# Expert numbers loaded two a slot behind up and down products, and matrix copies held until the up product of slot 10, in a two-stage mixture-of-experts kernel

## The reference

```python
def bitlinear(x, w):
    wq = w + jax.lax.stop_gradient(_weight_quant(w) - w)
    xq = x + jax.lax.stop_gradient(_act_quant(x) - x)
    return xq @ wq.T
...
idx = jnp.argmax(logits, axis=-1).reshape(-1)
for e in range(E):
    g = bitlinear(xf, wg[e])
    u = bitlinear(xf, wu[e])
    y = bitlinear(jnp.square(jax.nn.relu(g)) * u, wd[e])
    out = out + jnp.where((idx == e)[:, None], y, 0.0)
```

## Time and profile before

| | |
|---|---|
| median of three runs | 247.35 us (246.73 to 247.69) |
| the profiled execution | 247.17 us, of which the span of the profile is 245.3 us |
| busy in the span | TensorE 218.7 us (89%), VectorE 209.0 (85%), ScalarE 197.7 (81%), POOL 160.4 (65%) |
| first stage, up to the last product of block 18 | until about 169 us |
| loop over slots, gate 3 to gate 19 | about 182.6 to 232 us |
| last output write issued | 240.5 us |

### The profile page before, as it was taken

The page is one execution under the profiler, slowest core; times in us unless marked ns, Lnnn a source line. Parts: engine busy times, 40 slices in busy tenths (PEclk is TensorE's granted clock), DMA queues, the critical chain, the costliest instruction groups (busy, mean ns, idle before and its releaser), DMA issues.

```text
span 245.3 us, 6263 instructions
## 1 busy us (share of the span) xinstructions
PE 218.7 (89%) x1622; PEld 170.4 (69%) x1629; DVE 209.0 (85%) x696; ACT 197.7 (81%) x297; POOL 160.4 (65%) x324
## 2 busy tenths in 40 slices
PE   2398999999999999999999999987789999899970
PEld 2245688889899999999999998976334544343430
DVE  5969999977969899899988999979799998888771
ACT  2757799877768889998999979896678998788860
POOL 5262667756637598888987887553734878557762
PEclk9999999999999999999999999999979999999998
DMA  5999999996985266679565786335328899994120
GB/s 199 426 319 383 413 421 385 402 378 187 392 302 174 81 263 218 254 261 339 166 245 212 251 252 220 95 122 178 97 50 241 289 293 366 379 387 190 65 108 13
DMA packets 14273, 61.44 MB, mean 250 GB/s; under 512 B 2654, under 2 KB 2654, under 8 KB 9632
## 3 DMA queue, kind: packets, MB, share of 16 engines
q1 hardware_dynamic: 9600, 47.60, 53.6%
q0 software_dynamic: 4640, 13.44, 15.6%
HBM read 43.88 MB, written 12.70 MB: 231 GB/s over the span
## 4 chain that ended last, share of the span: by engine, by line
PE 68%; DVE 14%; DMA 7%; issue 6%; ACT 3%; POOL 1%; DVEq 0%; ACTq 0%; POOLq 0%
PE banks L1834 35%; PE banks L2014 15%; PE banks L1817 7%; DMA ternary<-weight_chunks 4%; PE banks L2016 4%; DMA x<-x_rows,gather 2%; PE banks L2003 2%; PE banks L1979 2%; PE banks L1859 2%; POOL out_rows L778 1%; DVE stats L1249 1%; DVE row L1305 1%; PE banks L1887 1%; DVE ternary L1108 1%; DVE p L1285 1%
## 5 line engine op out<-in xcount | busy, mean ns | idle before, releaser
L833 ACT ACTIVATE ternary<-staged 128x2048 bf16<-128x2048 f32 x20 | 38.1, 1906 | 1.8 <-DMA staged<-weight_chunks 1.8
L2014 PE MATMUL banks<-ternary,qT 128*128 x126 | 34.6, 394 | 3.3 <-ACT qT L922 1.6
L839 ACT ACTIVATE ternary<-staged,w_scale 128x1536 int16<-128x1536 f32 (+1 forms) x20 | 34.4, 1724 | 2.9 <-DVE w_scale L1202 2.9
L692 POOL DMA_INDIRECT x_rows<-row,store_at x19 | 22.3, 1172 | 9.3 <-POOL store_at L684 6.9
L1834 PE MATMUL banks<-ctx_hi,pT_hi 128*128 x132 | 23.0, 313 | 1.7 <-DVE row L1305 1.1
L594 POOL DMA_INDIRECT x<-x_rows,gather x16 | 18.3, 1145 | 9.2 <-DVE gather L1120 6.3
L647 POOL TENSOR_TENSOR row<-ln,half_powers 128x2 f32<-128x2 f32 x19 | 14.1, 744 | 14.9 <-DVE squares L1320 14.9
L2014 PEld LDWEIGHTS banks<-ternary,qT 128*128 128x128 bf16 x128 | 12.4, 101 | 16.4 <-issue 8.5
L1834 PE MATMUL banks<-ctx_hi,hT_hi 128*128 x132 | 22.8, 312 | 0.0
L1834 PE MATMUL banks<-ctx_lo,hT_hi 128*128 x132 | 21.2, 300 | 0.2 <-DVE ctx_lo L1149 0.2
L1834 PE MATMUL banks<-ctx_hi,pT_lo 128*128 x132 | 21.3, 301 | 0.0
(11 more groups left out here) (284 smaller groups left out, 641.0 us busy)
## 6 DMA issues: line engine op xcount, KB each, us to landing
staged<-weight_chunks SPq DMA_DIRECT2D x20, 1024.0 KB
twin<-ternary SPq DMA_DIRECT2D x4, 1536.0 KB
ternary<-ctx_chunks SPq DMA_DIRECT2D x4, 1024.0 KB, 7.9
ternary<-weight_chunks SPq DMA_DIRECT2D x4, 1024.0 KB, 12.3
ternary<-ctx_rows SPq DMA_DIRECT2D x4, 1024.0 KB, 11.0
late_rows<-x_rows SPq DMA_DIRECT2D x11, 260.0 KB, 3.0
x_rows<-filler SPq DMA_DIRECT2D x1, 2080.0 KB
staged<-x_rows SPq DMA_DIRECT2D x5, 260.0 KB, 3.5
```

The source lines that it names most:

```text
L692: pool.indirect_dma_start(x1_rows, bass.IndirectOffsetOnAxis(ap=store_at[b % ROWS][:, :], axis=0), row[b % ROWS][:, :], None, bounds_check ...
L833: nc.scalar.activation(ternary[:, m * K * D:(m + 1) * K * D], staged_of(i), ACT.Abs, accum_out=abs_sum[:, 2 * i:2 * i + 1]).then_inc(abs_r ...
L839: nc.scalar.activation(ternary[:, m * K * D + first:(m + 1) * K * D].bitcast(I16), staged_of(i)[:, first:], ACT.Copy, scale=w_scale[:, m:m ...
L2014: last = pe.matmul(ps[:, :], rows, ternary[:, columns], start=(k == 0), stop=(k == K - 1))
```

## The change

Three things are moved, none is added to the work.

1. `load_ffn_expert` leaves the gate products. In the loop over `u`, behind `up_product(u)` the number of slot u+1 is loaded for u < 5, and of slot 2u-3 from u = 5 on; behind `down_product(u-3)` that of slot 2u-2 is loaded from u = 4 on, and both only while there is such a slot. So slot 4 loads numbers 5 and 6, slots 5 to 10 load 7 to 18, two each, and slot 11 loads 19.
2. SP issues all eight half loads of slots 16 to 19 in a row, then loads the four numbers of the copies.
3. It then waits until `u_ready` is 11 (`NUMBERS`), which is when the up product of slot 10 is done, and issues the four copies one behind the other.

```diff
+NUMBERS = (B2 + EARLY) // 2 - 1
...
-            def copy_matrices(s):
+            def second_expert(s):
                 place = s - EARLY + SECOND
-                e = sp.value_load(expert2[1][place:place + 1, 0:1], min_val=0, max_val=E2 - 1)
+                return sp.value_load(expert2[1][place:place + 1, 0:1], min_val=0, max_val=E2 - 1)
+
+            def copy_matrices(s, e):
                 sp.dma_start(twin[s - SPLIT][:, :], ternary[:, bass.ds(e * (3 * K * D), 3 * K * D)])\
                     .then_inc(twin_in[s - SPLIT], 16)
...
             for s in range(SPLIT, B2):
                 for half in range(2):
                     load_half(s, half)
-                copy_matrices(s)
+            seconds = [second_expert(s) for s in range(SPLIT, B2)]
+            sp.wait_ge(u_ready, NUMBERS)
+            for s in range(SPLIT, B2):
+                copy_matrices(s, seconds[s - SPLIT])
...
             def gate_product(b):
...
-                ahead = None
-                if b >= EARLY:
-                    def ahead():
-                        load_ffn_expert(b + 1)
...
-                product2(g_ps[b % 2], qT[b % 2], b, 0, ahead=ahead).then_inc(g_ready, 1)
+                product2(g_ps[b % 2], qT[b % 2], b, 0).then_inc(g_ready, 1)
...
                 up_product(u)
-                if u < EARLY:
-                    load_ffn_expert(u + 1)
+
+                load_ffn_expert(u + 1 if u < EARLY else 2 * u - EARLY + 2)
                 if u == EARLY - 1:
                     spread_means(1)
                     transpose_q(u + 1)
                 transpose_r(u - 2)
                 down_product(u - 3)
+                if u >= EARLY - 1:
+                    load_ffn_expert(2 * u - EARLY + 3)
```

## The result

The changed kernel takes 249.75 us (median of 12 runs, 248.31 to 252.25); the kernel before, on the same chip, 247.07 (12 runs, 246.24 to 247.69). The ratio is 1.0113, 95% interval 1.0087 to 1.0138. 244.5 was forecast, so the time lies 3.5 us above the end of the range.

The account below looks back on a forecast made before the run. TensorE, 68% of the chain of waits, bounds the kernel, with stalls at number loads. 247.17 - 2.9 (stalls gone) + 0.1 (loads 18 and 19) = 244.4, 244.5 on the median's footing; range 243.9 to 246.2.

Parts of the forecast that it names:

- The excess at number loads: Gates 5 to 18: number loads, stretched by copies, leave 3.02 us of excess; moving them wins 2.9 us.
- They come back two a slot ... I take nothing: Behind up and down, slots 4 to 11: 14 loads of about 0.65 us hide under waits, cost nothing.
- My bounds, nothing and 0.20 a load: Moved number loads: nothing each by gates 6 to 8, 0.20 each by gate 5, 2.8 us in all.
- two loads a slot eat the lead: Rival, TensorE's instructions fall behind the array: 0.1 a load gives 245.9 us, 0.20 gives 247.3; chance 0.13.
- SP's row loads come together: SP: eight half loads at about 0.84 us end at 201.3, four numbers by 203.1 to 204.1.
- The copies must be there in time: SP's queue: 6.29 MB at 262 to 325 GB/s end between 223.7 and 228.3, all hidden, 0.3 to 5 us spare.
- the last copy is late: Rival: the fourth copy ends at 230.3, gate 19 waits 1.7 us, time 246.2; chance 0.07.
- In order: SP's queue: the four copies land one after another, each a quarter of the span after the one before.
- sharing of the queue: Rival: four copies share SP's queue, the first lands with the last, gate 16 stands 5 to 9 us, 250 to 253; chance 0.03.
- The wait for slot 10: SP reaches its wait just as up product 10 ends; nothing but the copies stands behind it.
- the cases for "faster": Below 246.1 us: all hidden (0.73), two thirds of the first rival, half of the second; given as 0.84.

Follow-up runs that it names:

- e9: Changed kernel without the four copies and TensorE's wait for them, second halves reading fixed matrices (output not the reference's); 245.46 us, ratio 0.9905 to 0.9955.
- e10: e3 without the four copies and TensorE's wait for them, second halves reading fixed matrices (output not the reference's); 244.13 us, ratio 0.9862 to 0.9933.
- e13: Changed kernel with each copy issued only when the one before it has landed; 253.34 us, ratio 1.0228 to 1.0292.
- e6: Changed kernel without SP's wait for up product 10 ahead of the copies; 250.88 us, ratio 1.0099 to 1.0199.
- e5: Changed kernel with each copy cut into two transfers of 64 partitions; 257.30 us, ratio 1.0356 to 1.0481.
- e3: Kernel before with each late number load moved from the middle of a gate to behind the up product, one a slot; 246.01 us, ratio 0.9977.
- e8: e3 with the first copy held until up product 8; 245.58 us, ratio 0.9947.
- e12: e4 with the first copy held until up product 9 in place of 10; 246.66 us, ratio 0.9979.
- e2: Kernel before with the changed kernel's SP order (copies together, held), number loads still in the gates; 249.17 us, ratio 1.0056 to 1.0112.
- e4: Changed kernel with half loads of slots 17 to 19 between the copies again, first copy held until up product 10; 247.25 us, ratio 1.0003.
- e7: e4 with the first copy held until up product 8 in place of 10; 249.36 us, ratio 1.0050 to 1.0123.
- e11: e7 with only one number load a slot, behind the up product, from slot 9 on; 247.35 us, ratio 0.9988 to 1.0034.
- e14: e3 with the first copy held until up product 9; 247.51 us, ratio 0.9952 to 1.0033.
- e1: Changed kernel's TensorE with the SP of before, half loads and copies interleaved without a hold; 249.07 us, ratio 1.0041 to 1.0130.

## Why the prediction was wrong, step by step

**The excess at number loads: right.** Taken away it gave 2.68 us in slots 9 to 15 where 2.8 were claimed, and loads beside copies are the cause: without copies the longest of 28 took 0.60 us (e9, e10), with them a kernel's median was 0.94 to 1.29.

**"They come back two a slot ... I take nothing": wrong in the kernel as run.** +1.58 us in slots 5 to 8 of the profiled execution, where others with the same order lost less. My bounds, nothing and 0.20 a load, were taken from a gate where the load was quiet. I gave a load 0.65 us where the trace has 0.30 and allowed for no long ones without a copy, though nothing forbade them. And each load under the wait for r or qT stood behind the other instructions of the slot: by the ten traces above the lead is used up with two quiet loads, so that every further tenth shows. The rival "two loads a slot eat the lead" was the mechanism, with a price per load where it should have had one per long load.

**"SP's row loads come together", 0.84 us each, end at 201.3: wrong in size.** 10.66 us for the eight; the first copy left at 206.7, not at 204.3. I had taken 0.39 for an issue and 0.45 for what lies between two, from one pair of 1.23 us. In the run an issue took 0.48, and between two lay (10.66 - 8 x 0.48) / 7 = 0.97 us: the read itself is only part of it. That is 2.4 us of delay for the first copy.

**"The copies must be there in time": wrong in size.** I took 262 to 325 GB/s, with the end at 223.7 to 228.3. From the first issue to the last landing it was 233.06 - 206.70 = 26.4 us for 6.29 MB, 239 GB/s; from the first packet (208.3) to the last landing 24.8 us, 254 GB/s. It wasn't the change that slowed them, since the kernel before had 25.7 us from the first copy packet to the end of the last and the changed kernel 24.2. The windows were the wrong measure: the earlier trace rows starts behind the first copy and ends ahead of the last one's end, and of its 5.20 MB only 4.53 are packets of copies (369 of 12288 bytes), 283 GB/s. My longest estimate was 24.0 us, so 2.4 us were missing here and 2.4 at SP's row loads. Either alone would have landed the last copy at 230.7, 0.6 us after gate 19 could have begun (220.27 + 9.82 = 230.1); together they are the 3.0 us of its wait. The rival "the last copy is late" had this at 0.07 with 1.7 us; it was 3.2.

**In order: right.** The copies landed at 214.2, 220.0, 226.7 and 233.1; gates 16 and 17 didn't wait, gate 18 came 0.1 us late. No sharing of the queue.

**The wait for slot 10: right** that it costs nothing, since SP came later.

So two of my rivals came together and their prices were added: -2.68 + 1.58 + 3.21. I had weighed each only alone, against the whole gain. (The shares of the cases for "faster" add up to 0.85, not 0.84; nothing hangs on it.)

## What to carry to other kernels

A small read of a table by an engine's instruction stream cost its quiet time only while little else was moving; beside a bulk copy it took three to four times that in the median and up to 5.7 times (1.70 us against 0.30), and beside output rows in some cases two to three times. Count on one such load in a gap, not two. Holding a bulk transfer back is paid at its other end: work out its last landing from the whole span that the same transfers took before, from first packet to last, and from the issuing engine's whole list of instructions, before asking what the hold buys. A rate from a window in the middle, or the time of a packet, doesn't give that span: here packets of 475 to 668 ns and packets of 640 to 654 ns made spans of 25.7 and 24.2 us.

## What was not expected of the hardware

**The clock falls at a wait, in some executions.** In e13 TensorE stood 3.83 us before gate 19; the granted clock in the rows by stretch (us, busy times, PEclk, DMA share, GB/s) was then 0.57 on average, at half speed for part of the stretch, so between its levels of 2.4 and 1.2 GHz:

```profile
232.00:236.00 4.00, 0.25 (x4) 0.24 (x5) 1.78 (x5) 0.37 (x1) 1.42 (x2) 1.00 0.86 272
236.00:240.00 4.00, 4.00 (x24) 1.59 (x22) 0.69 (x1) 2.22 (x4) 0.00 (x0) 0.57 0.15 55
```

From gate 19 to the span's end e13 took 15.3 us and e6, with a clock of 0.57 behind a wait of 2.58, 15.3, where before took 13.8. e5's two waits of over 4 us were both followed by such a fall. The changed kernel waited 3.01 us and kept its full clock (13.8). A late transfer so costs its wait, and in some executions 1.5 us more. It would explain why the median of the changed kernel lies above its profiled execution. That one had a mean granted clock of 0.996 over its span, and two others of the twelve had 0.997; these three took 248.31 to 249.79 us, median 248.87. The other nine had 0.978 to 0.989 and took 249.21 to 252.25, median 250.56. Where in those runs the clock fell no trace shows.

**The same happens earlier in most of the traces.** In before the clock fell from 178.3 to 181.8, ahead of a wait for VectorE that took up the lost time (0.41 us of it were left, in e9 1.97); in e9 it fell behind that wait, from 183.1 to 186.5:

```profile
178.00:182.00 4.00, 3.72 (x12) 1.46 (x12) 3.69 (x24) 2.49 (x5) 0.84 (x3) 0.57 0.02 2
```
```profile
184.00:186.00 2.00, 1.78 (x6) 0.66 (x5) 1.93 (x9) 0.97 (x2) 0.03 (x1) 0.50 0.79 247
```

Before, e3, e5, e8, e10, e12 and e13 are of the first kind, with gate 5 at 186.7 to 188.0; e2, e4, e6, e7, e9, e11 and e14 of the second, with gate 5 at 188.7 to 189.3; the changed kernel and e1 had no fall there. What decides it wasn't found. It is worth over a microsecond, as much as what most of these edits win or lose. Of the 1.6 us between the profiled executions of e9 and e10 the start of gate 5 makes 1.3 and the slots 0.24; whether their medians differ by 1.3 us for the same reason no trace shows.
